# Turning the attention output on VectorE in 32x32 squares instead of on TensorE

## The reference

```python
q = (x @ Wq + bq)  # 16 heads of 16, in 4 groups of 4
k = (x @ Wk + bk)  # 4 groups of 16
v = (x @ Wv + bv)  # 4 groups of 16
scores = q @ k.T / sqrt(16)          # key j is seen by query i if i - 128 < j <= i
out = softmax(scores) @ v            # (tokens, 256)
x = layernorm(x + out @ Wo + bo)
xr = mu_r * x + (1 - mu_r) * x_prev
xk = mu_k * x + (1 - mu_k) * x_prev
x = layernorm(x + sigmoid(xr @ W_r) * (relu(xk @ W_k) ** 2 @ W_v))
```

## Time and profile before

| | us |
|---|---|
| median of 3 runs | 453.26 |
| lowest and highest run | 449.74, 453.81 |
| span of the profiled execution | 449.1 |
| PE busy in it | 407.7 (91%) |
| DVE busy | 344.6 (77%) |
| POOL busy | 291.2 (65%) |
| ACT busy | 272.8 (61%) |

### The profile page before, as it was taken

How to read it: one execution, slowest core, us unless ns; L and a number is a source line. 1 busy time by engine, 2 the same in 40 slices (tenths; PEclk the granted TensorE clock), 3 DMA queues, 4 the chain that set the end, 5 groups by cost and what they waited for, 6 DMA issues and landing times.

```text
span 449.1 us, 8432 instructions
## 1 busy us (share of the span) xinstructions
PE 407.7 (91%) x2542; PEld 251.9 (56%) x2542; DVE 344.6 (77%) x852; ACT 272.8 (61%) x566; POOL 291.2 (65%) x466
## 2 busy tenths in 40 slices
PE   8976999997999979997999979997999979999853
PEld 3444546664556656564556665564656656665532
DVE  5765775898678976899688986799878988996551
ACT  2512567775667747764677657666577657778522
POOL 4552666776487856677487766688487767876531
PEclk9986899998999989999999989999999989999995
DMA  8484585412733175321753146421823144000000
GB/s 324 115 141 91 134 148 138 100 49 46 140 101 84 50 94 146 82 66 43 110 163 86 49 74 152 87 60 47 120 65 94 49 62 70 14 13 27 12 23 23
DMA packets 50892, 39.25 MB, mean 87 GB/s; under 512 B 33696, under 2 KB 42400, under 8 KB 50720
## 3 DMA queue, kind: packets, MB, share of 16 engines
q1 hardware_dynamic: 50416, 37.93, 38.9%
q10 hardware_dynamic: 432, 0.79, 0.6%
HBM read 26.38 MB, written 12.06 MB: 86 GB/s over the span
## 4 chain that ended last, share of the span: by engine, by line
PE 64%; DVE 19%; ACT 6%; issue 6%; DMA 2%; POOL 1%; SPq 1%; ACTq 0%; DVEq 0%; POOLq 0%
PE av_ps L983 11%; PE score_ps L969 9%; PE proj_ps L893 8%; PE max_ps L952 6%; PE gen L1070 6%; PE gen L1024 6%; PE gen L1081 5%; PE gen L1059 4%; DVE neg_max L704 4%; DVE q_tiles L696 3%; DVE max_parts L711 3%; PE max_ps L943 3%; ACT parts L517 2%; DVE mix L780 2%; PE av_ps L1040 2%
## 5 line engine op out<-in xcount | busy, mean ns | idle before, releaser
L410 POOL TENSOR_SCALAR_AFFINE_SELECT probs<-probs 128x512 f32<-128x512 f32 x252 | 168.2, 678 | 108.0 <-ACT probs L535 105.7
L535 ACT ACTIVATE probs<-score_ps 128x512 f32<-128x512 f32 x252 | 148.4, 598 | 86.0 <-PE score_ps L969 85.6
L969 PE MATMUL score_ps<-qs,ks 98*128 98x512 bf16 x252 | 99.8, 398 | 2.2 <-ACT probs L535 1.4
L704 DVE TENSOR_REDUCE neg_max<-max_ps 128x3 f32<-128x480 f32 x144 | 87.4, 631 | 12.3 <-PE max_ps L952 12.1
L983 PE MATMUL av_ps<-probs,vals 128*32 128x512 f32 x504 | 67.0, 605 | 0.9 <-POOL probs L410 0.8
L969 PEld LDWEIGHTS score_ps<-qs,ks 98*128 98x128 bf16 x252 | 25.0, 100 | 57.3 <-ACT probs L535 47.9
L1070 PE MATMUL gen<-mix,rest_w 128*128 128x128 f32 x256 | 38.7, 299 | 16.9 <-DVE mix L780 15.5
L952 PE MATMUL max_ps<-ks,q_tiles 96*128 96x160 bf16 x416 | 52.3, 243 | 0.0
L417 POOL TENSOR_TENSOR rstd<-var,minus_half 128x1 f32<-128x1 f32 x64 | 35.7, 558 | 21.7 <-DVE var L728 20.8
L1070 PEld LDWEIGHTS gen<-mix,rest_w 128*128 128x128 f32 x256 | 35.4, 208 | 22.7 <-DVE mix L780 17.8
L780 DVE SCALAR_TENSOR_TENSOR mix<-diff,first,x_t 128x128 f32<-128x128 f32 x128 | 43.8, 385 | 0.0
(11 more groups left out here) (86 smaller groups left out, 663.2 us busy)
## 6 DMA issues: line engine op xcount, KB each, us to landing
qs<-q_parts SPq DMA_DIRECT2D x48, 192.0 KB, 6.1
q_parts<-parts SPq DMA_DIRECT2D x48, 128.0 KB, 2.2
x_t<-x_feat SPq DMA_DIRECT2D x8, 512.0 KB, 3.7
x_in<-x_nat SPq DMA_DIRECT2D x8, 512.0 KB, 4.5
out<-out_t SPq DMA_DIRECT2D x32, 128.0 KB, 2.0
ks<-k_parts SPq DMA_DIRECT2D x42, 80.0 KB, 2.9
qs<-q_parts SPq DMA_DIRECT2D x42, 64.0 KB, 2.2
k_parts<-parts SPq DMA_DIRECT2D x8, 192.0 KB, 2.8
```

Source lines behind the costliest of these rows:

```text
L410: nc.gpsimd.affine_select(out=v, in_=v, compare_op=ALU.is_ge if i % 2 else ALU.is_gt, fill=0.0, base=0, pattern=[[0, HPG], [sign, BLK]], c ...
L535: nc.scalar.activation(probs[:, buf, i], score_ps[i % 2][:, :], ACT.Exp, scale=SCALE).then_inc(s_exp, 1)
L704: nc.vector.tensor_reduce(neg_max[:, TPB * i:TPB * i + n], max_bank(t, j, i)[:, 0:n * TILE_KEYS].rearrange("p (n k) -> p n k", k=TILE_KEYS ...
L969: nc.tensor.matmul(score_ps[i % 2][:, :].rearrange("p (h q) -> p h q", q=BLK), ks[0:ROWS + MPARTS, par, g, k0:k0 + BLK], qs[0:ROWS + MPART ...
```

## The change

The turning is given to VectorE, whose transpose turns each 32x32 square of a tile by itself. One transpose brings `av_ps` (PSUM) to `att_q` (SBUF), where the queries of a subblock of 32 are the partitions and each square has 32 columns (16 values, the sum, zeros). Reciprocal and product are as before, but read `att_q` in SBUF. A second transpose turns `att` to `att_c`. Since squares only are turned, the order of features in `att_c` is another, and the rows of `Wo` are permuted on the host to match. TensorE's `turn_back` and `turn_attention` and ScalarE's `att_t_copy` and `att_c_copy` are gone. `normalise` stands at its old place in DVE's order and waits for `s_av` (the product with the values) in place of `s_atr`; `values` waits for the first transpose of the block before (`s_att_q`) in place of `s_att_c`.

```diff
-        att_t = sb("att_t", [P, HPG * BLK])
+        att_q = sb("att_q", [P, HPG * NSUB, VCOL])
         recip = sb("recip", [P, HEADS])
-        att = sb("att", [P, D])
+        att = sb("att", [P, NSUB, HPG, DH])
...
-                if f1:
-                    att_t_copy()
...
-                if f1:
-                    att_c_copy()
...
                 def normalise():
 
-                    dve.wait_ge(s_atr, t)
-                    acc = av_ps[:, :].rearrange("p (h g v) -> p h g v", h=HPG, v=VCOL)
-                    rc = recip[:, :].rearrange("p (h g v) -> p h g v", h=HPG, v=1)
-                    nc.vector.reciprocal(rc, acc[:, :, :, DH:DH + 1]).then_inc(s_recip, 1)
-
+                    dve.wait_ge(s_av, t)
+                    nc.vector.transpose(att_q[:, :, :].rearrange("p b v -> p (b v)"), av_ps[:, :]).then_inc(s_att_q, 1)
+                    dve.wait_ge(s_att_q, t)
+                    nc.vector.reciprocal(recip[:, :].unsqueeze(2), att_q[:, :, DH:DH + 1]).then_inc(s_recip, 1)
                     dve.wait_ge(s_recip, t)
+                    nc.vector.tensor_tensor(att[:, :, :, :].rearrange("p n h d -> p h n d"),
+                                            att_q[:, :, 0:DH].rearrange("p (h n) d -> p h n d", n=NSUB),
+                                            recip[:, :].rearrange("p (h n) -> p h n", n=NSUB).unsqueeze(3)
+                                            .to_broadcast([P, HPG, NSUB, DH]), ALU.mult).then_inc(s_att, 1)
+                    dve.wait_ge(s_att, t)
                     if t >= 2:
 
-                        dve.wait_ge(s_ctr, t - 1)
-                    nc.vector.tensor_tensor(att[:, :].rearrange("p (g h v) -> p h g v", g=GROUPS, v=DH),
-                                            acc[:, :, :, 0:DH], rc.to_broadcast([P, HPG, GROUPS, DH]),
-                                            ALU.mult).then_inc(s_att, 1)
+                        dve.wait_ge(s_wo_ps, t - 1)
+                    nc.vector.transpose(att_c[:, :, :].rearrange("p c (n q) -> p n c q", q=SUB),
+                                        att[:, :, :, :].rearrange("p n (c h) d -> p n c (h d)", c=DC)).then_inc(s_att_c, 1)
...
                     if later(t, 1):
 
-                        pe.wait_ge(s_att_c, t)
+                        pe.wait_ge(s_att_q, t - 1)
...
-                if f1:
-                    turn_back()
...
-                if f1:
-                    turn_attention()
...
-    halves = [given("L0_attn_Wo")] + [given(n).T for n in ("L0_ffn_W_r", "L0_ffn_W_k", "L0_ffn_W_v")]
+    wo = given("L0_attn_Wo").reshape(GROUPS, 2, 2, DH, D).swapaxes(0, 1).reshape(D, D)
+    halves = [wo] + [given(n).T for n in ("L0_ffn_W_r", "L0_ffn_W_k", "L0_ffn_W_v")]
```

More of the change, by code:

```diff
@@ L190, in attention_channel_mix @@
         s_av = sem("s_av")
-        s_att_t = sem("s_att_t")
-        s_atr = sem("s_atr")
+        s_att_q = sem("s_att_q")
         s_recip = sem("s_recip")
         s_att = sem("s_att")
-        s_ctr = sem("s_ctr")
         s_att_c = sem("s_att_c")
@@ L562, in step @@
                 f1, f2, f3, f5 = (behind(t, j, scores, n) for n in (1, 2, 3, 5))
[L564 to L573, removed]
                 def first_norm(u):
@@ L1034, in turn_x2 @@
                     ins.then_inc(s_x2tr, 1)
[L1036 to L1050, removed]
                 def r_product(u):
```

## The result

The changed kernel takes 470.58 us (median of three executions; 468.78 to 474.19), against 451.8 us for the kernel before on the same chip: a ratio of 1.041, with an interval of 1.032 to 1.049. It is slower, as forecast, by 18.8 us where I had said about 10, and within the range of 450 to 477.

What follows compares the result with a forecast made beforehand. PE and DVE were taken as within 4% of each other, with DVE bounding after the change. Terms of -1.0, +9.0, +3.0 and -0.7 us gave +10.3, span 459.4, plus 4.2 to the median: 463 us, range 450 to 477 (0.81).

Steps and rivals of the forecast that it cites:

- The transposes: In `normalise` on DVE: 0.70 us for the first, plus 0.04 for dependence; 0.37 for the second after overlap.
- that rival (488): A 32-bit element costs the transpose two turns: 0.8 us more in each of 31 steps, 488 us; chance 0.08.
- The addition: DVE's extra work per step from transposes, reciprocal and product, less the old 0.63 us: 1.16 us.
- Waiting for GpSimd: The product with two SBUF inputs can wait for GpSimd's masks: 0.1 us net per step, bounds -0.2 and +0.4.
- The superblocks: Six superblocks of four steps with projections: DVE's addition less its fillable waits, +1.5 us each, +9.0 in all.
- 3.47 us of DVE's fillable waits: Four DVE waits in a superblock that shrink when DVE has more to do: 1.24 + 0.34 + 1.58 + 0.31 us.
- The clock: Rival: PE waits longer for DVE, one more clock fall in each superblock adds 10 us, 474 us; chance 0.11.
- the likeliest case: DVE bounds the kernel at the forecast prices: between 457.5 and 469 us, chance 0.45.
- The plain steps: Four steps without projections behind the superblocks: 10.8 us against 9.92, +3.0 us in all.
- The last steps: Steps drained one after the other at the end: one turn less on the way, -0.7 us.
- The start: Two steps before the first superblock in full flow: PE bounds and gains, -1.0 us.
- PE stays the bound (441): Rival: DVE's addition stays under 0.87 us a step and the kernel gets faster, 441 us; chance 0.11.

Runs made afterwards that it cites:

- recip_psum: The changed kernel with the 16 reciprocals written to the free attention bank in PSUM, so the product has one input in SBUF: 471.95 us, 1.038 of the kernel before.
- tile_first: The changed kernel with DVE's copy to `q_tiles` (`tile_q`) put ahead of `normalise`: 464.69 us, 1.015 of the kernel before.
- before_dve_more: The kernel before with two extra DVE transposes a step, from a constant tile to a spare one, PE and ScalarE still turning: 471.11 us, ratio 1.036.
- pe_load_back: The changed kernel with PE's six 128x128 products a step put back as idle work that nothing reads: 471.15 us, 1.036 of the kernel before.
- pe_saving_only: The kernel before with the turning left out and nothing in its place, so its result is no attention output: 449.89 us, ratio 0.987.

## Why the prediction was right in sign and short in size

- **The transposes** were priced right: 0.71 us for the first (0.70 forecast) and 0.45 for the second (0.43 forecast, before the overlap), so an element of 32 bits costs one turn, not two, and that rival (488) is out. The reciprocal took 0.25, not 0.182: I used L726 where `normalise` itself had one of 0.26. The addition is 1.23 us in place of 1.16.
- **Waiting for GpSimd** was priced right at 0.1 us a step. Against the earlier trace rows and the other groups of the trace before, `mixed` pays 3.6 us more over the whole kernel, the product 2.1 and the cast of `turn_max` 1.3, while `tile_q`, the second residual's `y` and the second step of `turn_max` pay 4.0 less: 3.0 us in 31 steps. The Trainium skill, "SBUF — State Buffer", section "Who interferes with whom", is borne out for the product: with two inputs in SBUF it took up to 895 ns, with one 420 to 422. But `recip_psum` shows that the rule can't be priced one instruction at a time, since the copy behind the product paid 4.6 us more.
- **The superblocks** are where it failed: +9.0 forecast, +18.1 measured (326.6 against 308.5 us for six). Two steps of the working were wrong. First, "Behind `normalise` on DVE stand `tile_q`, the second residual, `val_copy` and the next `tile_max`; PE waits for the last two" left out that PE waits for `tile_q` too, and first of all. `tile_first` shows the price of that order: 8.7 us. Second, I subtracted all of the 3.47 us of DVE's fillable waits. DVE's work in a superblock grew by 5.3 us (42.4 to 47.7), as priced (4.6 and 0.4). But DVE's idle time in a superblock only went from 7.6 or 9.3 us to 6.8, since PE, late itself, was late with what DVE waits for (`y` L816: 9.2 us over the kernel, 3.9 before).
- **The clock** was given as a rival of its own, 474, and what it forecast came: one more fall in each superblock, behind a wait of 2.4 us and one of 3.0, each followed by a stretch at 0.50 to 0.57. Its price was too high. I took the 1.7 us of the kernel before for each; it was 0.4 to 1.3 where DVE is late, and a superblock at the full clock lost 2.7 to 3.15 us all the same. So the loss is DVE's lateness in the main, and that 470.6 lies near the rival's 474 is luck. My argument against the rival held as far as it went: `before_dve_more` has a superblock at 1.00 with waits of 1.2 us for `q_tiles`. The wrong part was the bound on how long PE would wait ("up to 1.2 us each").
- **The range** held the result, but the likeliest case ended at 469 and did not. That the time lies within 450 to 477 owes as much to the width kept for the rivals as to the sum.
- **The plain steps** came as forecast: +2.3 us for +3.0, and a full step 11.09 us for 10.8. The last steps gave back 1.8 us for 0.7.
- **The start** went the other way: +4.9 us where I had -1.0. In the profiled execution the granted clock is 0.61 in 50 to 60 us, where it was 1.00 before. In 40 to 50 us it is low in both (0.71 now, 0.61 before), but in the kernel before it rose again and in the changed one it stayed down. `pe_load_back` was at 1.00 again from 50 us on. PE's waits in 40 to 50 us are 0.8 us at most in all three, so what decides this is left open.
- **PE's gain** was bounded by 20 us and measured at 4.8 in `pe_saving_only`, at nothing that can be told from 0 beside DVE's addition (`pe_load_back`). That PE stays the bound (441) needed an addition under 0.87 us, and it was 1.23.

The terms of the profiled execution add up: 4.9 + 18.1 + 2.3 - 1.8 = 23.5, and 472.6 - 449.1 = 23.5.

## What to carry to other kernels

When two engines are within a few per cent of each other in the steps that set the pace, work that moves from one to the other must be priced at the place where it lands: list everything behind it on its new engine, and for each item who waits for it. Time that is taken from an engine that already waits for the other comes back as a longer wait. The longest of these waits were mostly followed by a lower clock of TensorE, and here each such fall cost 0.4 to 1.7 us. Before a change like this one, look for the stall that both engines share: moving a single GpSimd instruction by one step was worth 4.6%, more than the whole question of who turns the attention output. And read the superblocks before the medians: the clock of the first and last steps moved the total by up to 5 us for reasons that no experiment here aimed at.

## What the runs showed of the hardware

- VectorE's transpose of 32-bit data took 0.71 us for 128x512 out of PSUM and 0.45 for 128x256 in SBUF. With L718's 0.211 for 32 elements, that is close to 1 ns per element of a partition and 0.18 us on top.
- Four 128x128 identity products of 32-bit data within a stream of matmuls cost TensorE 0.43 us and two of them 0.22. So at the full clock TensorE did in 0.65 us, with two copies by ScalarE on the side, what added 1.23 us to VectorE.
- The clock fell behind waits of 2.36 and 3.00 us in the changed kernel and read 0.50 to 0.57 for a stretch of 2 to 3 us behind them. The length of a wait does not decide it alone: a wait of about 2.6 us was followed by no fall in the superblock 270.35 to 320.40, which kept 1.00, nor was one of 3.00 us in `tile_first`. One such fall cost 1.7 us between two superblocks of the earlier trace rows, 0.8 and 1.3 in `pe_load_back`, 0.7 in `before_dve_more` and 0.4 in `tile_first`.
- An addition of one element per partition, moved from DVE to GpSimd, freed 1.3 us of DVE's 374 and not its own 9.8 (64 times 0.153), because `mixed`, beside which GpSimd now does it, went from 424 to 520 ns in the mean. In the kernel with TensorE's turning it freed nothing: `mixed` went from 363 to 489 ns and DVE's busy time from 339.9 to 341.8 us.
